# Routing weights turned and expanded by short products, GpSimd's product of unit 10 moved up, last output blocks evacuated between scans

## The chip, the cores and the metric

The kernel runs on one core of a Trainium2 chip. The metric is the device time of one execution in microseconds (us); the times before are the median of three runs. Engines are named as in the profile: PE is TensorE (PEld its weight loads), DVE is VectorE, ACT is ScalarE, POOL is GpSimd, SP is the engine that issues most DMAs.

## What is computed

The output is `x + ffn(mix(x, f, cond))`, in float32, for 4 batches of 1024 tokens by 1024 channels. The reference, cut to what matters:

```python
# mix: r = x, k = v = f, tf = sigmoid(sum(cond)) per batch
ek = exp(min(k, 30)); ekv = ek * v
nf, nb = scan(ekv), reverse_scan(ekv)          # a = a * decay + ekv_t, over the tokens
df, db = scan(ek), reverse_scan(ek)
euk = exp(min(u + k, 30))
y = sigmoid(r) * (nf + nb - ekv + euk * v) / max(df + db - ek + euk, 1e-8) * (0.8 + 0.2 * tf)
# ffn on y
h = silu(y @ rw1.T + rb1)
logits = h @ rw2.T + rb2 + gates               # 16 experts
coeff = softmax of the two largest logits, scattered to a row of 16, zero elsewhere
xa = einsum('ni,eri->ner', y, A)               # rank 16 per expert, so 256 values per token
out = x + y @ W.T + bias + einsum('ner,eor->no', xa * coeff[:, :, None], B)
```

## The kernel before

**Layout.** Everything is channel major: a tile has 128 channels on the partitions and tokens along the free dimension. A *unit* is one batch and one block of 128 channels (1024 tokens): 32 units, eight per batch, one per step `s` of the loop that every engine runs. A *group* `G` is one batch's half of 512 tokens: 8 groups; its outputs are eight blocks `j` of 128 channels.

**The recurrences (DVE, POOL, ACT).** For a unit DVE runs four scans of about 2.2 us each: forward of the denominator (L704) and of the numerator (L708), backward of both (L713, L734); and between them L718 (product with v), L723 (sum of the denominators), L692 (scaling of the next unit's exponential) and L747 (the ratio, which gives y). POOL makes the numerator's input of the next unit (`p1`, L602, which DVE's next forward scan waits for), sums the numerators (L580, after the backward scan), gates them (L586, which L747 waits for), and takes the remainder of y (L612). ACT does exponentials, sigmoids, logarithms with table loads between them, and rounds y.

**Products in three passes.** Each product is done in a rounded type (fp32r) with both operands split into a rounded part and a remainder: hi*hi, hi*lo, lo*hi. `y_hi` is ACT's, `y_lo` is POOL's (L612), and TensorE waits for `y_lo` of a unit. A 128x512 product is one instruction. ffn's output blocks accumulate in five PSUM banks; `acc` holds them.

**Routing of a group.** TensorE makes the hidden layer (`hid`, L936) and xa (`low_rank`), and then the logits (`logits`, L974). DVE's `routing` finds the two largest and their weights with some twenty small instructions, tokens on the partitions. The weights must then multiply xa, which has the 256 (expert, rank) rows on the partitions. Before, `fan_out` (L810) writes each weight 16 times, to `fan`, 128x512 twice; TensorE turns `fan` against an identity in full float32 (`spread`, L981), eight products of 128x128, which run as sixteen instructions. DVE multiplies (`weigh`, L818), ACT rounds the result (`split_wx`, L470), POOL takes its remainder (`wx_lo`, L625), and then TensorE runs `expert`. It waits for `wx_lo` before the first of them. Between `spread` and `expert` it has base products of the third output block, 24 of them in groups 2 to 7, and twelve more.

**Order.** Each engine's program is written by hand as a loop over steps, with tables that place work of groups 0 and 1 (`routing_at`, `weigh_at`, `evacs_at`) and rules for groups 2 to 7 (`quarter`, `ends_at`). Every engine runs strictly in that order and waits at semaphores. Group 0 is routed in step 9, group 1 in step 12; group G from 2 on in step 8+4G+1, and its last five output blocks are evacuated (L754, `evacuate`) in step 8+4G+4. Banks that are evacuated are taken by the next group's first products (`bank_in`).

## Time and profile before

| | |
|---|---|
| median of 3 runs | 689.52 us (688.38 to 690.01) |
| the profiled execution, its own time | 688.6 us |
| its span, first to last instruction | 686.6 us |
| PE busy | 598.7 us (87%) |
| DVE busy | 526.6 us (77%) |
| POOL busy | 368.1 us (54%) |
| ACT busy | 357.1 us (52%) |
| mean granted clock of TensorE | 0.957 |

Busy time is an average over stages. In the first 250 us or so DVE has little idle time and PE waits; later PE runs almost without a gap while DVE ends its scans at 537 us.

### The profile page before, as it was taken

The page shows a single profiled execution, that of the slowest core. Times are in us where ns is not written, and L with a number is a line of the kernel's source. Part 1 is how long each engine was busy: PE and PEld are TensorE (multiplying, and loading weights), DVE is VectorE, ACT ScalarE, POOL GpSimd, SP SyncE. Part 2 cuts the span into 40 slices and gives each one's busy share as a digit, 9 for nine tenths or more (in the row PEclk, how much of TensorE's full clock was granted, in tenths as well). Part 3 has the DMA queues.
Part 4 walks back from the last instruction along what each step waited for, and adds up shares of the span by engine and source line. Part 5 has one row for each costly group of instructions (what it writes and reads, how often), then busy time and mean ns, then how long its engine had stood idle before and what let it go on. Part 6 is the DMA issues. An engine that isn't in the chain of part 4 may idle for free.

```text
span 686.6 us, 7030 instructions
## 1 busy us (share of the span) xinstructions
PE 598.7 (87%) x2626; PEld 490.1 (71%) x2626; DVE 526.6 (77%) x573; ACT 357.1 (52%) x418; POOL 368.1 (54%) x183
## 2 busy tenths in 40 slices
PE   0153588989999937999999999999999999999997
PEld 0132466768878825887888878888888888888886
DVE  7999999999999999998899797979897532021202
ACT  4777789785656666655655554656465420011000
POOL 1789997867868876647544753565465501000100
PEclk9976799989999978999999999999999999999999
DMA  5323476522945831234423360427132402040022
GB/s 190 122 90 121 124 254 205 194 100 71 215 107 121 203 113 64 74 113 160 141 73 113 109 198 32 153 63 242 33 116 84 124 29 66 27 153 1 25 67 76
DMA packets 33169, 78.42 MB, mean 114 GB/s; under 512 B 4720, under 2 KB 4848, under 8 KB 33136
## 3 DMA queue, kind: packets, MB, share of 16 engines
q1 hardware_dynamic: 30832, 73.79, 33.2%
q0 software_dynamic: 2304, 4.20, 3.8%
q8 instruction: 20, 0.33, 0.2%
q14 instruction: 13, 0.11, 0.0%
HBM read 57.00 MB, written 20.97 MB: 114 GB/s over the span
## 4 chain that ended last, share of the span: by engine, by line
PE 49%; DVE 25%; POOL 16%; issue 7%; ACT 1%; DMA 1%; SPq 0%; DVEq 0%; POOLq 0%; ACTq 0%
PE acc L925 15%; PE acc L927 15%; PE acc L926 15%; DVE mix L713 5%; POOL mix L602 4%; POOL kv L580 4%; POOL yr L586 4%; DVE yr L747 3%; DVE mix L708 3%; DVE eu L723 3%; DVE kv L718 2%; DVE xo L754 2%; POOL y_lo L612 2%; DVE mix L734 2%; PE acc L936 1%
## 5 line engine op out<-in xcount | busy, mean ns | idle before, releaser
L925 PE MATMUL acc<-y_hi,wa_hi 128*128 128x512 f32 x640 | 258.5, 404 | 59.7 <-POOL y_lo L612 52.7
L926 PE MATMUL acc<-y_lo,wa_hi 128*128 128x512 f32 x640 | 255.3, 399 | 0.0
L927 PE MATMUL acc<-y_hi,wa_lo 128*128 128x512 f32 x640 | 254.8, 398 | 0.0
L925 PEld LDWEIGHTS acc<-y_hi,wa_hi 128*128 128x128 f32 x640 | 124.1, 194 | 89.3 <-POOL y_lo L612 54.1
L927 PEld LDWEIGHTS acc<-y_hi,wa_lo 128*128 128x128 f32 x640 | 123.8, 194 | 26.7
L926 PEld LDWEIGHTS acc<-y_lo,wa_hi 128*128 128x128 f32 x640 | 124.2, 194 | 25.6
L602 POOL TENSOR_TENSOR mix<-mix,kv 128x1024 f32<-128x1024 f32 x31 | 74.3, 2397 | 75.7 <-DVE mix L692 59.4
L754 DVE SCALAR_TENSOR_TENSOR xo<-acc,bias_sb,xo 128x512 f32<-128x512 f32 x64 | 46.4, 735 | 75.2 <-PE acc L927 75.2
L612 POOL TENSOR_TENSOR y_lo<-yr,y_hi 128x1024 fp32r<-128x1024 f32 x31 | 74.3, 2398 | 50.2 <-ACT y_hi L402 50.2
L625 POOL TENSOR_TENSOR wx_lo<-xa,wx_hi 128x512 fp32r<-128x512 f32 x16 | 20.9, 1329 | 129.3 <-ACT wx_hi L470 129.3
L580 POOL TENSOR_TENSOR kv<-mix,kv 128x1024 f32<-128x1024 f32 (+1 forms) x32 | 75.4, 2356 | 5.3 <-DVE mix L734 5.3
L704 DVE TENSOR_TENSOR_SCAN mix<-d_ps,mix 128x1024 f32<-128x1024 f32 x32 | 73.1, 2284 | 5.8 <-POOL mix L602 5.7
L414 ACT ACTIVATE mix<-mix,rdelta_g 128x1 f32<-128x1 f32 x64 | 18.6, 296 | 111.6 <-DVE mix L708 71.6
L586 POOL TENSOR_TENSOR yr<-kv,yr 128x1024 f32<-128x1024 f32 (+1 forms) x32 | 75.2, 2351 | 2.5
L713 DVE TENSOR_TENSOR_SCAN mix<-d_ps,mix 128x1023 f32<-128x1023 f32 x32 | 74.8, 2336 | 0.3 <-ACT mix L414 0.3
L734 DVE TENSOR_TENSOR_SCAN mix<-d_ps,mix 128x1023 f32<-128x1023 f32 (+1 forms) x32 | 73.7, 2303 | 0.0
L708 DVE TENSOR_TENSOR_SCAN mix<-d_ps,mix 128x1024 f32<-128x1024 f32 x32 | 72.7, 2272 | 0.0
L402 ACT ACTIVATE y_hi<-yr 128x1024 fp32r<-128x1024 f32 x31 | 32.9, 1060 | 51.6 <-DVE yr L747 51.6
L747 DVE SCALAR_TENSOR_TENSOR yr<-eu,limit_g,yr 128x1024 f32<-128x1024 f32 (+1 forms) x32 | 40.2, 1257 | 22.5 <-POOL yr L586 22.5
L925 PE MATMUL acc<-wx_hi,wb_hi 128*128 128x512 f32 x128 | 50.0, 391 | 1.8 <-POOL wx_lo L625 1.8
L926 PE MATMUL acc<-wx_lo,wb_hi 128*128 128x512 f32 x128 | 49.8, 389 | 0.0
L927 PE MATMUL acc<-wx_hi,wb_lo 128*128 128x512 f32 x128 | 49.8, 389 | 0.0
(98 smaller groups left out, 738.3 us busy)
## 6 DMA issues: line engine op xcount, KB each, us to landing
kv<-f_cm SPq DMA_DIRECT2D x32, 512.0 KB, 3.6
yr<-x_cm SPq DMA_DIRECT2D x32, 512.0 KB, 3.4
out<-xo SPq DMA_DIRECT2D x64, 256.0 KB, 4.2
xo<-x_cm SPq DMA_DIRECT2D x64, 256.0 KB, 3.9
out<-xo POOLq DMA_DIRECT2D x16, 256.0 KB, 6.8
xa<-w_base SPq DMA_DIRECT2D x5, 512.0 KB, 3.5
xo<-w_base SPq DMA_DIRECT2D x3, 512.0 KB, 5.7
xo<-w_router_a SPq DMA_DIRECT2D x2, 480.0 KB, 3.6
```

The source lines that it names most:

```text
L580: nc.gpsimd.tensor_tensor(kv[:, g % 2, t], num_of(g)[:, t], kv[:, g % 2, t], ALU.add).then_inc(n_ready, 1)
L586: nc.gpsimd.tensor_tensor(yr[:, g % 2, t], kv[:, g % 2, t], yr[:, g % 2, t], ALU.mult).then_inc(gated, 1)
L602: nc.gpsimd.tensor_tensor(num_of(g), den_of(g), kv[:, g % 2, :], ALU.mult).then_inc(p1_ready, 1)
L612: nc.gpsimd.tensor_tensor(slots(y_lo, g), yr[:, g % 2, :].rearrange("p (h t) -> p h t", h=2), slots(y_hi, g).bitcast(fp32), ALU.subtract). ...
L704: nc.vector.tensor_tensor_scan(den_of(g), decay(g, T), den_of(g), 0.0, ALU.mult, ALU.add).then_inc(den_fwd, 1)
L708: nc.vector.tensor_tensor_scan(num_of(g), decay(g, T), num_of(g), 0.0, ALU.mult, ALU.add).then_inc(num_fwd, 1)
L713: nc.vector.tensor_tensor_scan(rev(den_of(g)), decay(g, T - 1), rev(den_of(g)), den_of(g)[:, T - 1:T], ALU.mult, ALU.add).then_inc(den_bwd, 1)
L734: nc.vector.tensor_tensor_scan(a[:, stop - 1::-1], decay(g, stop), a[:, stop - 1::-1], a[:, stop:stop + 1], ALU.mult, ALU.add).then_inc(nu ...
L747: nc.vector.scalar_tensor_tensor(out=yr[:, g % 2, t], in0=eu[:, t], scalar=limit_f[:, g:g + 1], in1=yr[:, g % 2, t], op0=ALU.min, op1=ALU. ...
L925: nc.tensor.matmul(out_ap, wh, yh, start=start, stop=False)
L926: nc.tensor.matmul(out_ap, wh, yl, start=False, stop=False)
L927: return nc.tensor.matmul(out_ap, wl, yh, start=False, stop=stop)
```

## The change

The routing weights of a group are no longer written 16 times each. DVE adds the two hits into one row of 16 weights per token, writes a rounded copy of it twice and its remainder twice side by side into `cat` (128 tokens by 4x2x32), TensorE turns `cat` in the rounded type (`turn`, four products of 64 columns of weights by 128), ACT copies the result from PSUM to `cat_t` (64x512), and TensorE expands it (`spread`, two products of 32 rows by 512 columns with a constant 0/1 matrix `expand`). For groups 1 to 7 nine base products stand between `turn` and `spread`; for group 0 none. The identity and the 0/1 matrix are rounded once on ACT in step 3.

In step 9, DVE weighs xa of group 0 after the sum of the denominators instead of before it, and POOL does `p1(10)` ahead of the two `wx_lo` of group 0. The last five blocks of groups 2 to 6 are evacuated one step earlier, between the instructions of the scans (one of them at the start of the step after). `u` is read without a copy per batch.

```diff
+        last_blocks_at = {(-1, AFTER_BWD_DEN): 3, (-1, AFTER_P2): 4, (-1, AFTER_SUM): 5, (-1, AFTER_SCALE): 6,
+                          (0, AFTER_FWD): 7}
-        weigh_at = {(CB + 1, AFTER_P2): 0, (CB + 4, AFTER_RATIO): 1}
+        weigh_at = {(CB + 1, AFTER_SUM): 0, (CB + 4, AFTER_RATIO): 1}
...
@@ ACT
+            def constants():
+                act.wait_ge(late_in, 16 * 8)
+                nc.scalar.activation(ident_r[:], ident_raw, ACT.Copy).then_inc(constants_ready, 1)
+                nc.scalar.activation(expand_r[:], expand_raw, ACT.Copy).then_inc(constants_ready, 1)
+
+            def copy_turned(G):
+                act.wait_ge(turned, G + 1)
+                nc.scalar.activation(cat_t[:], acc[0:4 * E, banks[G][0], :], ACT.Copy).then_inc(cat_t_ready, 1)
...
+                if q == 1:
+                    copy_turned(G)
                 if s == CB + 4:
                     exp_gap(1)
                     copy_xa(1)
+                    copy_turned(1)
...
+                if s == 3:
+                    constants()
+                if s == CB + 1:
+                    copy_turned(0)
@@ POOL
-                if s in (CB + 1, CB + 4):
-                    split_wx((s - CB) // 4)
+                if s == CB + 4:
+                    split_wx(1)
                 if s + 1 < UNITS:
                     p1(s + 1)
+                if s == CB + 1:
+                    split_wx(0)
@@ DVE
-                for a in range(2):
-                    fan_out(a)
...
+                nc.vector.tensor_tensor(second_hit, first_hit[:, :, :], second_hit, ALU.add).then_inc(route, 1)
+                twice = second_hit.unsqueeze(2).to_broadcast([P, TPG, 2, E])
+                routed_to(11 + 2 * TPG)
+                nc.vector.tensor_copy(cat[:, :, :, 0:E], twice).then_inc(route, 1)
+                routed_to(12 + 2 * TPG)
+                nc.vector.tensor_tensor(cat[:, :, :, E:2 * E], twice, cat[:, :, :, 0:E].bitcast(fp32),
+                                        ALU.subtract).then_inc(cat_ready, 1)
...
+            def last_blocks(s, place):
+                for late in (-1, 0):
+                    G = ends_at.get(s - late, -1)
+                    if SPLIT <= G < GROUPS - 1 and (late, place) in last_blocks_at:
+                        evacuate(G, last_blocks_at[late, place])
@@ PE
-            def spread(G, a):
-                pe.wait_ge(fan_ready, 2 * G + a + 1)
-                for t in range(TPG):
-                    last = nc.tensor.matmul(acc[:, banks[G][2 * a], t * P:(t + 1) * P], fan[:, a, t * P:(t + 1) * P], ident_sb[:],
-                                            start=True, stop=True)
-                last.then_inc(c_done, 1)
+            def turn(G):
+                pe.wait_ge(cat_ready, G + 1)
+                for t in range(TPG):
+                    last = nc.tensor.matmul(acc[0:4 * E, banks[G][0], t * P:(t + 1) * P],
+                                            cat[:, t, :, :].rearrange("p a k -> p (a k)"), ident_r[:], start=True, stop=True)
+                last.then_inc(turned, 1)
+
+            def spread(G):
+                pe.wait_ge(cat_t_ready, G + 1)
+                for a in range(2):
+                    rows = slice(2 * E * a, 2 * E * (a + 1))
+                    nc.tensor.matmul(acc[:, banks[G][2 * a], :], expand_r[rows, :], cat_t[rows, :],
+                                     start=True, stop=True).then_inc(c_done, 1)
...
+                turn(G)
                 pe.wait_ge(xa_copied, 2 * G + 2)
-                for a in range(2):
-                    spread(G, a)
                 if G:
-                    for kc in range(k0, CB):
+                    for kc in range(k0, k0 + 3):
+                        base(G, 2, kc)
+                spread(G)
+                if G:
+                    for kc in range(k0 + 3, CB):
                         base(G, 2, kc)
```

On POOL, in step 9. `wb_lo` is the remainder of the last weights, `mix<-mix,kv` is `p1(10)`, and `kv<-mix,kv` the sum of unit 9's numerators. Before:

```order
L573 TENSOR_TENSOR wb_lo<-xo,wb_hi 128x1024
L625 TENSOR_TENSOR wx_lo<-xa,wx_hi 128x512 x2
L602 TENSOR_TENSOR mix<-mix,kv 128x1024
L580 TENSOR_TENSOR kv<-mix,kv 128x1024
L586 TENSOR_TENSOR yr<-kv,yr 128x1024
```

and in the changed kernel:

```order
L598 TENSOR_TENSOR wb_lo<-xo,wb_hi 128x1024
L627 TENSOR_TENSOR mix<-mix,kv 128x1024
L650 TENSOR_TENSOR wx_lo<-xa,wx_hi 128x512 x2
L605 TENSOR_TENSOR kv<-mix,kv 128x1024
L611 TENSOR_TENSOR yr<-kv,yr 128x1024
```

The product of unit 10 has gone ahead of the two remainders.

On ACT, in the same step. `ex` is the exponential of the routing, `wb_hi` the last weights, `yr<-yr` the sigmoid of unit 9 between its two table loads. Before:

```order
L465 ACTIVATE ex<-gap 128x4
L446 ACTIVATE wb_hi<-xo 128x1024
L426 ACT_TABLE_LOAD
L426 ACTIVATE yr<-yr 128x1024
L478 ACT_TABLE_LOAD
L470 ACTIVATE wx_hi<-xa 128x512 x2
```

and in the changed kernel:

```order
L472 ACTIVATE ex<-gap 128x4
L453 ACTIVATE wb_hi<-xo 128x1024
L481 ACTIVATE cat_t<-acc 64x512
L433 ACT_TABLE_LOAD
L433 ACTIVATE yr<-yr 128x1024
L496 ACT_TABLE_LOAD
L486 ACTIVATE wx_hi<-xa 128x512 x2
```

The copy of the turned weights, which waits for TensorE, stands ahead of both table loads and the sigmoid, and `wx_hi` behind them as it did.

On DVE, steps 19 and 20, where group 2 ends (`xo<-acc` is an evacuated block, `mix` a scan). Before, from the backward scan of unit 19's denominator:

```order
L713 SCALAR_TENSOR_TENSOR mix<-d_ps,mix 128x1023
L718 SCALAR_TENSOR_TENSOR kv<-eu,kv 128x1024
L723 SCALAR_TENSOR_TENSOR eu<-eu,mix 128x1024
L692 TENSOR_SCALAR mix<-mix,delta_g 128x1024
L734 SCALAR_TENSOR_TENSOR mix<-d_ps,mix 128x1023
L754 SCALAR_TENSOR_TENSOR xo<-acc,bias_sb,xo 128x512 x2
L704 SCALAR_TENSOR_TENSOR mix<-d_ps,mix 128x1024
L754 SCALAR_TENSOR_TENSOR xo<-acc,bias_sb,xo 128x512
L708 SCALAR_TENSOR_TENSOR mix<-d_ps,mix 128x1024
L754 SCALAR_TENSOR_TENSOR xo<-acc,bias_sb,xo 128x512
L747 SCALAR_TENSOR_TENSOR yr<-eu,limit_g,yr 128x1024
L754 SCALAR_TENSOR_TENSOR xo<-acc,bias_sb,xo 128x512
```

and in the changed kernel:

```order
L740 SCALAR_TENSOR_TENSOR mix<-d_ps,mix 128x1023
L781 SCALAR_TENSOR_TENSOR xo<-acc,bias_sb,xo 128x512
L745 SCALAR_TENSOR_TENSOR kv<-eu,kv 128x1024
L781 SCALAR_TENSOR_TENSOR xo<-acc,bias_sb,xo 128x512
L750 SCALAR_TENSOR_TENSOR eu<-eu,mix 128x1024
L781 SCALAR_TENSOR_TENSOR xo<-acc,bias_sb,xo 128x512
L719 TENSOR_SCALAR mix<-mix,delta_g 128x1024
L781 SCALAR_TENSOR_TENSOR xo<-acc,bias_sb,xo 128x512
L761 SCALAR_TENSOR_TENSOR mix<-d_ps,mix 128x1023
L731 SCALAR_TENSOR_TENSOR mix<-d_ps,mix 128x1024
L781 SCALAR_TENSOR_TENSOR xo<-acc,bias_sb,xo 128x512
L735 SCALAR_TENSOR_TENSOR mix<-d_ps,mix 128x1024
```

Four blocks now stand ahead of the backward scan of the numerator, where none stood, and five ahead of the ratio, where four stood.

## Rows read from the trace of the kernel before

**Rows 1.** The page: busy tenths of TensorE in 40 slices
```profile
PE   0153588989999937999999999999999999999997
```

**Rows 2.** Waits of TensorE: who waited for whom, us in total, times, longest
```profile
PE acc L925 <- POOL y_lo L612: 52.7, 4, 27.7
PE acc L936 <- POOL y_lo L612: 9.7, 2, 8.9
```

**Rows 3.** Timeline of TensorE, group 5: start, duration, row, idle before
```profile
487.12 1.06 PE L974 MATMUL acc<-rw_sb,fan 64*128 64x16 f32 x8
...
488.12 0.50 PE L925 MATMUL acc<-y_hi,wa_hi 128*128 128x512 f32 x1
...
493.69 1.95 PE L981 MATMUL acc<-ident_sb,fan 128*128 128x128 f32 x16
...
495.39 0.48 PE L925 MATMUL acc<-y_hi,wa_hi 128*128 128x512 f32 x1
```

**Rows 4.** Timeline of VectorE, step 9
```profile
147.84 1.28 DVE L810 TENSOR_TENSOR fan<-first_hit,d_ps 128x512 f32<-128x512 f32 x2
...
149.04 1.22 DVE L718 SCALAR_TENSOR_TENSOR kv<-eu,kv 128x1024 f32<-128x1024 f32 x1
...
152.81 0.74 DVE L692 TENSOR_SCALAR mix<-mix,delta_g 128x1024 f32<-128x1024 f32 x1
...
157.09 2.29 DVE L704 TENSOR_TENSOR_SCAN mix<-d_ps,mix 128x1024 f32<-128x1024 f32 x1 [1.27 <-POOL mix L602]
```

**Rows 5.** Timeline of ScalarE, steps 8 and 9
```profile
134.48 0.58 ACT L450 COPY fan<-acc 64x512 f32<-64x512 f32 x1
...
147.05 1.28 ACT L426 ACT_TABLE_LOAD   x1
...
150.91 0.63 ACT L470 ACTIVATE wx_hi<-xa 128x512 fp32r<-128x512 f32 x1 [0.21 <-DVE xa L818]
```

**Rows 6.** Timeline of GpSimd, step 9
```profile
151.62 3.07 POOL L625 TENSOR_TENSOR wx_lo<-xa,wx_hi 128x512 fp32r<-128x512 f32 x2 [2.11 <-ACT wx_hi L470]
...
154.65 2.41 POOL L602 TENSOR_TENSOR mix<-mix,kv 128x1024 f32<-128x1024 f32 x1
```

**Rows 7.** Timeline of TensorE, groups 0 and 1
```profile
139.41 1.86 PE L974 MATMUL acc<-rw_sb,fan 64*128 64x16 f32 x8 [2.45 <-DVE fan L764]
...
141.19 0.79 PE L925 MATMUL acc<-y_hi,wa_hi 128*128 128x512 f32 x1
...
149.09 1.95 PE L981 MATMUL acc<-ident_sb,fan 128*128 128x128 f32 x16
...
154.75 0.50 PE L925 MATMUL acc<-wx_hi,wb_hi 128*128 128x512 f32 x1 [0.80 <-POOL wx_lo L625]
...
197.85 1.95 PE L981 MATMUL acc<-ident_sb,fan 128*128 128x128 f32 x16
```

**Rows 8.** Stretch of TensorE after its wait at 139 us: busy, clock, DMA
```profile
141.19:149.09 7.90, 7.90 (x25) 0.69 0.40 133
```

**Rows 9.** Timeline of VectorE, step 12
```profile
192.38 0.22 DVE L775 TENSOR_TENSOR lg<-acc,rbg 128x64 f32<-128x64 f32 x1 [0.56 <-PE acc L974]
...
200.01 1.27 DVE L818 TENSOR_TENSOR xa<-acc,xa 128x512 f32<-128x512 f32 x2
```

**Rows 10.** Timeline of TensorE, first products of groups 2, 3, 4 and 6
```profile
250.09 0.79 PE L936 MATMUL acc<-y_hi,wr 128*128 128x512 f32 x1 [8.90 <-POOL y_lo L612]
...
321.77 0.50 PE L936 MATMUL acc<-y_hi,wr 128*128 128x512 f32 x1 [0.60 <-DVE xo L754]
...
404.96 0.50 PE L936 MATMUL acc<-y_hi,wr 128*128 128x512 f32 x1 [0.83 <-POOL y_lo L612]
...
548.99 0.39 PE L936 MATMUL acc<-y_hi,wr 128*128 128x512 f32 x1
```

**Rows 11.** Timeline of VectorE, step 32
```profile
537.44 2.70 DVE L754 SCALAR_TENSOR_TENSOR xo<-acc,bias_sb,xo 128x512 f32<-128x512 f32 x4
```

**Rows 12.** Timeline of GpSimd, step 32
```profile
545.05 2.39 POOL L612 TENSOR_TENSOR y_lo<-yr,y_hi 128x1024 fp32r<-128x1024 f32 x1 [2.56 <-ACT y_hi L402]
```

More of the change, by code:

```diff
@@ L8, in decay_mix_with_routed_lora_channel_major @@
 def decay_mix_with_routed_lora_channel_major(nc, x_cm, f_cm, cond, w, u, w_router_a, w_base, w_expert, bias, rb1, rw2,
-                                             rb2, gates, ident, iota, out):
+                                             rb2, gates, ident, expand, iota, out):
     fp32, fp32r, u32 = mybir.dt.float32, mybir.dt.float32r, mybir.dt.uint32
@@ L60, in decay_mix_with_routed_lora_channel_major @@
         wx_hi = nc.alloc_sbuf_tensor_at("wx_hi", [P, 2, N], fp32r, offset=fan_at)
-        ident_sb = sb("ident_sb", [P, P])
+        cat = nc.alloc_sbuf_tensor_at("cat", [P, TPG, 2, 2 * E], fp32r, offset=fan_at)
+        cat_t = nc.alloc_sbuf_tensor_at("cat_t", [4 * E, N], fp32r, offset=fan_at + 4 * N)
+        ident_r = sb("ident_r", [P, P], fp32r)
+        expand_r = sb("expand_r", [4 * E, P], fp32r)
         rw2_sb = sb("rw2_sb", [HID, E])
@@ L161, in base_from @@
             return HALF if G < SPLIT else 0
-        (AFTER_FWD, AFTER_FWD_NUM, AFTER_RATIO, AFTER_BWD_DEN, AFTER_P2, AFTER_SUM, AFTER_BWD_NUM) = range(7)
+        (AFTER_FWD, AFTER_FWD_NUM, AFTER_RATIO, AFTER_BWD_DEN, AFTER_P2, AFTER_SUM, AFTER_SCALE, AFTER_BWD_NUM) = range(8)
         hidden_at = {(CB, AFTER_BWD_NUM): 0, (CB + 3, AFTER_SUM): 1}
@@ L263, in decay_mix_with_routed_lora_channel_major @@
         ex_ready = sem("ex_ready")
-        fan_ready = sem("fan_ready")
+        cat_ready = sem("cat_ready")
+        turned = sem("turned")
+        cat_t_ready = sem("cat_t_ready")
+        constants_ready = sem("constants_ready")
         xa_done = sem("xa_done")
@@ L390, in exp_uk @@
                     act.wait_ge(y_ready, g)
-                nc.scalar.activation(eu[:], kv[:, g % 2, :], ACT.Exp, bias=u_f[:, g:g + 1]).then_inc(euk_ready, 1)
+                nc.scalar.activation(eu[:], kv[:, g % 2, :], ACT.Exp, bias=u_sb[:, g % CB:g % CB + 1]).then_inc(euk_ready, 1)
             def split_hi(g):
@@ L473, in drain_part @@
                 act.wait_ge(part_done, p + 1)
+                if p == PBUF - 1:
+                    act.wait_ge(constants_ready, 2)
                 if p >= PBUF:
@@ L490, in _ @@
             weights_hi(0)
-            act.wait_ge(u_ready, 1)
+            act.wait_ge(u_in, 16)
             for s in range(STEPS):
@@ L766, in routing @@
             def routing(G):
-                ROUTE = 10 + 2 * TPG
+                ROUTE = 12 + 2 * TPG
                 def routed_to(n):
@@ L803, in routing @@
                 routed_to(10 + 2 * TPG)
-                for a in range(2):
-                    fan_out(a)
-            def fan_out(a):
-                e = slice(a * P // RANK, (a + 1) * P // RANK)
-                wide = [P, TPG, P // RANK, RANK]
-                nc.vector.tensor_tensor(fan[:, a, :].rearrange("p (t e r) -> p t e r", t=TPG, r=RANK),
-                                        first_hit[:, :, e].unsqueeze(3).to_broadcast(wide),
-                                        second_hit[:, :, e].unsqueeze(3).to_broadcast(wide), ALU.add).then_inc(fan_ready, 1)
+                nc.vector.tensor_tensor(second_hit, first_hit[:, :, :], second_hit, ALU.add).then_inc(route, 1)
[5 more added lines that the diff above has]
+                                        ALU.subtract).then_inc(cat_ready, 1)
             def weigh(G):
@@ L859, in _ @@
                 ended = ends_at.get(s, -1)
-                ending = ended >= 0
+                ending = ended == GROUPS - 1
                 if ending:
@@ L873, in _ @@
                 first_groups(s, AFTER_FWD)
+                last_blocks(s, AFTER_FWD)
                 if ending:
@@ L907, in _ @@
                 first_groups(s, AFTER_BWD_DEN)
+                last_blocks(s, AFTER_BWD_DEN)
                 if s < UNITS:
@@ L910, in _ @@
                 first_groups(s, AFTER_P2)
+                last_blocks(s, AFTER_P2)
                 if s < UNITS:
@@ L913, in _ @@
                 first_groups(s, AFTER_SUM)
+                last_blocks(s, AFTER_SUM)
                 if s + 1 < UNITS:
                     scale_e(s + 1)
+                last_blocks(s, AFTER_SCALE)
                 if q == 0 and routed:
@@ L1034, in _ @@
                     if G == 0:
-                        pe.wait_ge(late_in, 16 * 7)
+                        pe.wait_ge(late_in, 16 * 8)
                 else:
@@ L1133 @@
         "ident": np.eye(P, dtype=np.float32),
+        "expand": np.concatenate([np.tile(h, (2, 1)) for h in np.split(np.repeat(np.eye(e, dtype=np.float32), r, axis=1), 2,
+                                                                       axis=1)]),
         "iota": np.arange(e, dtype=np.float32),
```

16 lines of the change are left out of this document (7 added, 9 removed).

## The prediction

> **What bounds the kernel now.** I read the page's slices first, then TensorE's waits, then the timelines of the places where the change acts. The slices [rows 1] show three stages: to about slice 5 TensorE works in bursts, then nearly always, with one dip at slices 14 and 15, and from there it is full to the end. The waits [rows 2] name what the bursts and the dip wait for: the remainder of y from GpSimd (L612), 52.7 us in four waits, and 9.7 us in two at the head of a group. So the first stages go at the pace of the unit chain (VectorE's scans with GpSimd between them), and that chain also sets when group 2 starts, at 250.09 after a wait of 8.90 [rows 10]. From there TensorE is the bound, with small waits: 0.60 for an evacuated block at 321.77 and 0.83 for a unit at 404.96 [rows 10].
>
> Two things follow. In groups 0 and 1 a change counts only by what it does to the unit chain. From group 2 on it counts by TensorE's own instructions, and by units that come too late.
>
> **TensorE's short products.** Before, a group's turn of the weights is sixteen instructions and the next product starts 1.70 us after their first (493.69 to 495.39) [rows 3], 0.106 each. The change puts 4 + 2 there. The two of 512 columns: 24 products between 488.12 and 493.69 [rows 3] take 0.23 each, so 0.46; 0.23 if both ran at once. The four short ones are a form the trace lacks. The nearest rows are the sixteen at 0.106 and the logits, eight at (488.12 - 487.12) = 0.125 though only 16 columns move [rows 3]. Half an 0.106 is the lower end (half the weight columns), 0.21 the upper (no gain from the type: two of today's instructions each). I take 0.11: 0.45 for four, ends 0.2 and 0.85. For changing between shapes I take 0.15 of the logits' excess, ends 0 and 0.3. Sum 1.06 (0.43 to 1.61), so a group saves 0.64 us (1.27 to 0.09).
>
> TensorEngine Tiling (Array Packing) in the Trainium skill, section Key Properties, says that changing the tiling mode drains TensorE, which speaks against splitting one block of short products into two of other shapes. The logits row, with its 0.125 for 16 columns, doesn't contradict it, and the 0.15 stands without it.
>
> **VectorE in the routing.** The two wide writes took 1.20 (147.84 to 149.04) [rows 4]. Three dependent ones of 64, 128 and 128 elements replace them: 0.4 by elements, 1.2 at most; I take 0.85. It saves 0.35 per group.
>
> **Group 0, step 9: the largest term.** Before: the turn starts at 149.09, as soon as the base products end, `wx_hi` at 150.91 [rows 5], `wx_lo` at 151.62 and the experts at 154.75 [rows 6, 7]. Now, in order:
> - `cat` is ready at 147.84 + 0.85 = 148.7; TensorE is free at 149.09, as before, and done at 149.7 with the way to PSUM.
> - ACT copies 64x512, which takes 0.58 [rows 5]: 150.3. Behind it in ACT's queue stand two table loads and the sigmoid, which ran unhindered from 147.05 and let `wx_hi` start 3.65 later (3.86 less its 0.21 of waiting) [rows 5]. So `wx_hi` starts at 150.3 + 3.65 = 153.95 and both halves are there at 155.1.
> - VectorE: from 149.04 to the scaling at 152.81 [rows 4] the same four instructions stand as now; from 148.7 with 0.2 less waiting that gives 152.3, and 153.0 when scaled.
> - GpSimd does `p1(10)`, 2.4 us [rows 6], to 155.4, and then the two remainders. They took 3.07 there; they cannot take less than the 2.4 of one full width. I take 2.7: 158.05. The experts start at 158.1 instead of 154.75, that is 3.3 later.
> - The clock. After the 2.45 us wait at 139.41 and the logits, the granted clock over the next 7.90 us was 0.69 of full, so partly at 1.2 GHz [rows 7, 8], and 24 products took 7.90 instead of 5.5. Here TensorE waits 0.7 for the copy, 0.7 for `xa`, and then nearly 4 us. The fall costs 0 to 2.4; I take 1.2. TensorE is 4.5 late.
>
> What is behind it: TensorE has no gap from there to the logits of group 1, and VectorE waited 0.56 for those at 192.38 [rows 9]. The scan of unit 10, which began at 157.09 after 1.27 of waiting for `p1` [rows 4], now begins at 155.5; but that 1.6 is lost again, first at the evacuation of group 0's first block, which needs the experts, and at the latest at those logits. So VectorE's chain is 4.5 late at 192, less 0.35 for the routing. Then `weigh(1)`: TensorE's turn at 197.85 [rows 7] + 4.5, 0.55 for turn and shape change, nine products 2.07, and 0.4 to the first result give 200.9 + 4.5; VectorE is ready at 200.01 - 0.35 + 4.5 [rows 9]. It waits 1.2. The chain is then 4.5 - 0.35 + 1.2 = 5.35 late, and has no slack up to the y that group 2 waits for. So group 2 starts 5.35 late (3.8 with the clock held, 6.6 at the other end).
>
> **Groups 2 to 7.** TensorE saves 0.64 in each, six times 3.8. The 0.60 wait at 321.77 goes, as block 3 is evacuated in time: four blocks, done within 2.7 us [rows 11], stand earlier. Its cover is that group 2's experts are done when VectorE comes by.
>
> What is late next is the unit that a group needs. In group 4 it was 0.83 late already. VectorE's steps 17 to 24 are locked to TensorE at the logits of group 3; behind these the chain gets +1.2 of waiting in `weigh`, -0.35, and one more block ahead of the ratio (0.65): 1.5. So TensorE loses 1.5 there and the saving of group 3 with it. In group 6, the last unit's y was ready at 545.05 + 2.39 = 547.44 and needed at 548.99 [rows 10, 12]. Now four blocks (2.6) stand ahead of its last scan, and +0.85 as before: 550.9. TensorE loses 1.9 and the saving of group 5.
>
> **Sum, against the profiled execution:** 5.35 - 0.60 - 0.64 (group 2) + 1.5 (to group 4) - 0.64 (4) + 1.9 (to group 6) - 1.28 (6 and 7) = +5.6 on 688.6, so 694.2; 695.1 against the median, which lies 0.9 above. I predict **694.5**, with 691 to 698 as this case's own range (the clock, the price of the short products, and units 1 us earlier).
>
> `u` without its copy, the two roundings in step 3, and one more small DMA cost nothing: the first scaling waits for ACT's exponential, and ACT has idle time in every step. With that cover gone they cost 0.2 to 0.5 once.
>
> **Rivals.**
> - *The savings count and the front does not stretch (faster).* Place: ACT's copy in step 9. If group 0's experts start less than about 0.5 us late (VectorE's slack at 192.38), the 1.6 of the scan of unit 10 and twice 0.35 stay in the chain. Then 688.6 - 2.3 - 3.8 - 0.6 + 1.2 = 683 to 685. For it: POOL and VectorE idle there before. Against: ACT's queue order and 3.65 us of table loads and sigmoid. I give it 0.22, at 685.
> - *The two expansions run at once.* They use rows 0 to 31 and 32 to 63. Then 0.23 less, seven times, as it also brings `weigh` forward: 692.9. TensorEngine Tiling (Array Packing), Key Properties, says that different tiles can execute in parallel; no row of this trace has two such tiles. Chance 0.12.
> - *Short products are not cheap* (0.21 each). Then 0.4 more in each of seven groups: 697.3. Chance 0.13.
> - *It cancels*: full clock in group 0, 3.8 there, units in time in groups 4 and 6 because the slack at the ratio takes the blocks: 688.6 + 3.8 - 0.6 - 3.8 = 688 to 690. Chance 0.10.
>
> The forecast keeps 0.43. Its neighbours on the slower side are 0.12 and 0.13. A measurement of this kernel can tell about 0.2%, 1.4 us, from no change. Faster: 0.20 of the first rival, 0.02 of the last. Same: 0.02, 0.08, and 0.05 from the forecast's and second rival's warm-clock ends, 0.15. Slower: 0.63. The range 685.5 to 698 leaves out about 0.12 of the first rival below and 0.06 above.
>
> **What would show it.** Right: `wx_lo` of group 0 starting behind `p1(10)` at about 155.4 and TensorE waiting 3 to 4 us for it; VectorE waiting 3 us or more at the first instruction of group 1's routing; about 1.2 us of waiting at `weigh` in groups 1 to 5; group 2's first product at 253 to 257; TensorE waiting 2 to 3 us for a unit in group 4 and 1 to 2 in group 6; steady groups at 71.3 instead of 71.9 us. Wrong: experts of group 0 at 156 or earlier; group 2 starting at 250 or earlier; four short products under 0.3 us or over 0.7.

## The result and the profile after

The changed kernel takes 695.94 us (median of five runs, 694.77 to 696.10) against 689.06 us (five runs, 688.38 to 690.01): a ratio of 1.0095, 95% interval 1.0081 to 1.0109. It is slower by 6.9 us, or 1%. Its profiled execution took 695.62 us, with a span of 693.5 us. All points of time below, unless said otherwise, are from the profiled executions (this one against 688.6 us with a span of 686.6 before).

The page's slices of TensorE (against [rows 1]; slices are counted from 0):

```profile
PE   0243688879999946999999989999999999999997
```

The dip at slices 14 and 15 is still there (4 and 6 for 3 and 7), and slice 23 has an 8 where a 9 stood: TensorE, full to the end before, now has a gap in group 4. Its waits (who for whom, us in all, times, longest), against [rows 2]:

```profile
PE acc L959 <- POOL y_lo L637: 53.4, 4, 27.5
PE acc L970 <- POOL y_lo L637: 16.3, 4, 9.9
PE acc L959 <- POOL wx_lo L650: 3.0, 2, 1.8
```

The wait for the first units is as it was. At the head of a group it is 16.3 us in four waits where it was 9.7 in two. The timeline of TensorE (start, duration, row, idle before) has the products that it waited for, against [rows 10]. They are not the first of their groups, as the heading of [rows 10] and the prediction call them (only the row of group 3 there is): in group 2 it is the first product of the batch's unit 6, and in groups 4 and 6 that of unit 7, the batch's last. "Group 2 starts" is kept below for the first of them.

```profile
254.88 0.80 PE L970 MATMUL acc<-y_hi,wr 128*128 128x512 f32 x1 [9.87 <-POOL y_lo L637]
...
409.19 0.50 PE L970 MATMUL acc<-y_hi,wr 128*128 128x512 f32 x1 [2.94 <-POOL y_lo L637]
...
555.75 0.50 PE L970 MATMUL acc<-y_hi,wr 128*128 128x512 f32 x1 [2.41 <-POOL y_lo L637]
```

They are 4.79, 4.23 and 6.76 us later than before. The start of each group's logits, for which the same products stand before and after, gives the shift between these points: +3.09 in group 3 (345.03 against 341.94), +5.80 in group 4 (421.00), +5.00 in group 5 (492.12), +8.49 in group 6 (567.54) and +7.68 in group 7. So two things act in turn: a late unit pushes TensorE back, and each group without one gives 0.81 us back (a period of 71.12 us, where it was 71.93). Between the late unit of group 4 and that group's logits another 1.57 us is lost, and 1.73 in group 6. The stretches of TensorE behind both units tell why; columns: window and its length, busy time (instructions), granted clock, DMA share, GB/s:

```profile
409.19:421.00 11.81, 11.81 (x45) 0.86 0.38 122
...
555.75:567.54 11.79, 11.79 (x44) 0.86 0.01 1
```

TensorE is busy all the time, but the granted clock is 0.86: part of each stretch ran at 1.2 instead of 2.4 GHz. Before, the same work took 10.24 us at 1.00:

```profile
404.96:415.20 10.24, 10.24 (x45) 1.00 0.19 60
```

The timeline of group 4 shows where in the stretch it was. From 410.22 to 413.62 eight products start 0.41 to 0.43 us apart, and behind them they start 0.23 apart again; eight times 0.20 is the 1.6 us. Two rows, one of each kind:

```profile
410.63 0.63 PE L959 MATMUL acc<-y_hi,wa_hi 128*128 128x512 f32 x1
...
413.87 0.40 PE L961 MATMUL acc<-y_hi,wa_lo 128*128 128x512 f32 x1
```

The short products, in group 5, against [rows 3]:

```profile
498.69 0.40 PE L1015 MATMUL acc<-ident_r,cat 128*64 128x128 f32 x4
498.92 0.45 PE L959 MATMUL acc<-y_hi,wa_hi 128*128 128x512 f32 x1
499.21 0.40 PE L960 MATMUL acc<-y_lo,wa_hi 128*128 128x512 f32 x1
...
500.83 0.40 PE L961 MATMUL acc<-y_hi,wa_lo 128*128 128x512 f32 x1
501.16 0.50 PE L1023 MATMUL acc<-cat_t,expand_r 32*128 32x512 f32 x2
501.59 0.50 PE L959 MATMUL acc<-y_hi,wa_hi 128*128 128x512 f32 x1
501.92 0.39 PE L960 MATMUL acc<-y_lo,wa_hi 128*128 128x512 f32 x1
```

Four turning products take 0.23 us from start to start, and the pair of expanding ones 0.43. Around them the spacing of the base products is a little wider than its usual 0.23: 0.29 behind the turn, 0.33 before and 0.33 behind the expansion. In all 0.30 us for the turn and 0.64 for the expansion, 0.94 a group. The sixteen of before took 1.70, and the product behind them stood 0.32 from the next instead of 0.23, so 1.79 in all.

Group 0, where the front comes from: ScalarE, GpSimd, VectorE and TensorE, against [rows 4 to 7]:

```profile
148.91 0.59 ACT L481 ACTIVATE cat_t<-acc 64x512 fp32r<-64x512 f32 x1 [2.29 <-PE acc L1015]
149.52 1.28 ACT L433 ACT_TABLE_LOAD   x1
150.82 1.06 ACT L433 ACTIVATE yr<-yr 128x1024 f32<-128x1024 f32 x1
151.89 1.28 ACT L496 ACT_TABLE_LOAD   x1
153.19 1.15 ACT L486 ACTIVATE wx_hi<-xa 128x512 fp32r<-128x512 f32 x2
```

```profile
152.50 2.39 POOL L627 TENSOR_TENSOR mix<-mix,kv 128x1024 f32<-128x1024 f32 x1 [3.44 <-DVE mix L719]
154.85 2.50 POOL L650 TENSOR_TENSOR wx_lo<-xa,wx_hi 128x512 fp32r<-128x512 f32 x2
```

```profile
154.93 2.29 DVE L731 TENSOR_TENSOR_SCAN mix<-d_ps,mix 128x1024 f32<-128x1024 f32 x1 [0.25 <-POOL mix L627]
160.20 0.75 DVE L781 SCALAR_TENSOR_TENSOR xo<-acc,bias_sb,xo 128x512 f32<-128x512 f32 x1 [2.98 <-PE acc L961]
```

```profile
157.41 0.62 PE L959 MATMUL acc<-wx_hi,wb_hi 128*128 128x512 f32 x1 [1.78 <-POOL wx_lo L650]
```

The copy of the turned weights ends at 149.50, and the table loads and the sigmoid behind it hold `wx_hi` back until 153.19. GpSimd's remainders follow its product, and the experts start at 157.41. The scan of unit 10 begins 2.2 us earlier than before, and VectorE then stands 2.98 us at the first evacuation.

### The profile page after: what moved, and what is told of

It reads as the page before. It is cut to its first block, busy times and chain, and to the rows that moved or that the text cites. A ratio compares the mean times of both kernels' runs of the same rounds, so it can differ in the third digit from the quotient of the medians.

```text
span 693.5 us, 6883 instructions
## 1 busy us (share of the span) xinstructions
PE 596.4 (86%) x2546; PEld 481.8 (69%) x2546; DVE 521.5 (75%) x580; ACT 361.9 (52%) x428; POOL 367.3 (53%) x183
## 4 chain that ended last, share of the span: by engine, by line
PE 51%; DVE 22%; POOL 17%; issue 7%; ACT 1%; DMA 0%; POOLq 0%; DVEq 0%; SPq 0%; ACTq 0%
PE acc L959 16%; PE acc L961 16%; PE acc L960 16%; DVE mix L740 5%; POOL mix L627 5%; POOL kv L605 4%; POOL yr L611 4%; DVE yr L774 3%; DVE eu L750 2%; POOL y_lo L637 2%; DVE kv L745 2%; DVE mix L735 2%; DVE xo L781 2%; DVE mix L731 2%; DVE mix L761 1%
```

## The experiments

The times are medians of 5 to 12 runs; the kernel before had 688.7 to 689.2 us beside them, and ratios are against it. The runs of a version spread by 1 to 5 us from lowest to highest run, so differences under 1 us say little. Two tables give all but experiments 2, 5, 6 and 10, in us ("blocks" are the last five output blocks of groups 2 to 6, which the expectations of experiments 3 and 4 call those of groups 2, 4 and 6; the edits move all five groups'):

| | last blocks in a row | blocks between scans |
|---|---|---|
| weights of before | 689.0 (before) | 694.0 |
| short products, orders of the change | 693.8 | 695.9 (after) |
| short products, both orders of group 0 mended | 690.4 | 691.7 |

| with the late units covered (below) | |
|---|---|
| before | 688.0 |
| blocks between scans alone | 687.9 |
| after | 686.1 |
| after, with the orders of group 0 mended and two units between | 683.6 |

**1. ScalarE's order in group 0**, on the changed kernel, with GpSimd's order put back too. (The expectation calls the moved work a copy of 64x512; it is `wx_hi`, two of 128x512.)

```diff
@@ ACT
                     copy_turned(0)
+                    split_wx(0)
...
-                if s == CB + 1:
-                    split_wx(0)
@@ POOL
-                if s == CB + 4:
-                    split_wx(1)
+                if s in (CB + 1, CB + 4):
+                    split_wx((s - CB) // 4)
                 if s + 1 < UNITS:
                     p1(s + 1)
-                if s == CB + 1:
-                    split_wx(0)
```

> Edit on the kernel after: for group 0 ScalarE's copy of 64x512 that splits the weighed remainder (wx) is put directly behind its copy of the turned weights, so that the two loads of activation tables and the sigmoid between come after it, and GpSimd forms the remainder of group 0 ahead of its product of unit 10, as before the change. Theory A (the late start of group 2 comes from ScalarE's order in group 0): in the kernel after, that copy started at 153.19, 4.3 us behind the turned weights' copy at 148.91; moved, it should start near 150.2-150.5, the experts' products of group 0 should start near 153.8-154.2 instead of 157.41, group 2's first product near 251.0-251.8 instead of 254.88, and the whole should come out 3 to 4.5 us under the kernel after (about 691.5-693), near 1.004 of the kernel before. Rival B (the delay is made later, in the routing steps of group 1 or by the clock, whatever the start of group 0): the experts start earlier but group 2's first product stays within 1 us of 254.88 and the time within 1 us of 695.9.

Measured: 691.74 us (690.89 to 695.74), ratio 1.005 [1.0031, 1.007], 4.2 under the changed kernel. On ScalarE and TensorE:

```profile
149.46 0.59 ACT L481 ACTIVATE cat_t<-acc 64x512 fp32r<-64x512 f32 x1 [2.29 <-PE acc L1012]
151.75 1.23 ACT L486 ACTIVATE wx_hi<-xa 128x512 fp32r<-128x512 f32 x2 [1.70 <-DVE xa L840]
153.00 1.28 ACT L433 ACT_TABLE_LOAD   x1
```

```profile
149.01 0.42 PE L1012 MATMUL acc<-ident_r,cat 128*64 128x128 f32 x4 [1.13 <-DVE cat L833]
150.20 0.49 PE L1020 MATMUL acc<-cat_t,expand_r 32*128 32x512 f32 x2 [0.77 <-ACT cat_t L481]
151.77 0.79 PE L956 MATMUL acc<-y_hi,wa_hi 128*128 128x512 f32 x1 [1.08 <-DVE xa L840]
...
251.87 0.79 PE L967 MATMUL acc<-y_hi,wr 128*128 128x512 f32 x1 [9.88 <-POOL y_lo L636]
```

`wx_hi` is 1.4 us earlier, not 3, since it now waits 1.70 for VectorE's `xa`. The experts start at 156.12, later than expected: nothing releases them any more, TensorE comes there by itself, with three waits of about 1 us in the step and seven of the twelve products behind them at half clock (0.43 apart). Group 2 starts at 251.87, 3.0 earlier than in the changed kernel's profile. Theory A holds for the place, with the start of the experts missed by 2 us. Its size is in part the clock: kernels with the changed kernel's group 0 but with the clock held behind the experts start group 2 at 253.7 (experiments 3, 5 and the third of 9), so the orders give 1.9 and that clock the other 1.1; and in group 4 the clock did not fall here behind a wait of 2.79 us (10.20 us from unit to logits), which is 1.6 more.

**2. GpSimd's order alone** (the part of that diff under POOL).

> Edit on the kernel after: only GpSimd's order is put back: the remainder of group 0 (wx_lo, two instructions) is formed ahead of the product of unit 10, as before the change; ScalarE's order stays as in the kernel after. Theory A (ScalarE's order sets the experts' start): wx_lo then waits for ScalarE's copy, which ends at 154.35, and can be done near 156.9 instead of 157.4; the experts start 0.3-0.9 us earlier, and unit 10's product about 4 us later, which puts its scan behind. The time comes out 0 to 1 us under the kernel after (695.0-695.9). Rival B (GpSimd's product standing ahead of the remainder is what delays the experts): the experts start near 154-155 and the time falls by 2.5 us or more.

Measured: 694.11 us (693.42 to 695.27), 1.8 under the changed kernel; experts at 156.83, group 2 at 252.82. The experts came 0.6 earlier, as A said; the time fell by more than A's 1 us and less than B's 2.5. Part of this may not be from the edit: the changed kernel's profiled execution lost 1.6 us more to the clock in group 0 (below). Against the 253.7 of the kernels with the clock held, group 2 starts 0.9 earlier here and 1.9 earlier in experiment 1, so each of the two orders costs about 1 us.

**3. The last blocks in a row again.**

```diff
-        last_blocks_at = {(-1, AFTER_BWD_DEN): 3, (-1, AFTER_P2): 4, (-1, AFTER_SUM): 5, (-1, AFTER_SCALE): 6,
-                          (0, AFTER_FWD): 7}
+        last_blocks_at = {}
...
-                ending = ended == GROUPS - 1
+                ending = ended >= 0
```

> Edit on the kernel after: the last accumulator blocks of groups 2, 4 and 6 are evacuated where they were before the change (in one row at the group's end), not between the scans. Theory A (the moved evacuations put the units of groups 4 and 6 off, TensorE waits 2.94 and 2.41 us for them, and its granted clock falls after both waits, 1.6-1.7 us each): the wait for a free accumulator at group 3's first product comes back (+0.6 to +0.8), the wait at group 6's unit falls under 0.7 and leaves no fall of the clock (-1.8 -1.7), the wait at group 4's unit falls by about 0.65 (-0.7), with its clock fall kept or gone (0 to -1.6): 3.0 to 5 us under the kernel after, 691-693. Rival B (the late units come from the late start of group 2 alone and the evacuations are neutral): the two waits stay as they are and the time is that of the kernel after plus 0.6-0.8, 696.6.

Measured: 693.84 us (691.98 to 695.06), 2.1 under the changed kernel, which is less than the 3 to 5 of theory A and the other way than B. The late units are gone as A said (0.78 us in group 4 and none in group 6), but another wait has come, on TensorE:

```profile
326.82 0.50 PE L969 MATMUL acc<-y_hi,wr 128*128 128x512 f32 x1 [1.23 <-DVE xo L780]
...
399.31 0.50 PE L969 MATMUL acc<-y_hi,wr 128*128 128x512 f32 x1 [1.07 <-DVE xo L780]
...
410.40 0.50 PE L969 MATMUL acc<-y_hi,wr 128*128 128x512 f32 x1 [0.78 <-POOL y_lo L636]
...
473.06 0.50 PE L969 MATMUL acc<-y_hi,wr 128*128 128x512 f32 x1 [1.20 <-DVE xo L780]
...
545.04 0.50 PE L969 MATMUL acc<-y_hi,wr 128*128 128x512 f32 x1 [0.56 <-DVE xo L780]
```

With the row kept, the 0.8 us that TensorE saves in a group makes it reach the next group's accumulators before VectorE has emptied them, and it hands the saving back there. So the two large parts of the change belong together: with the evacuations moved, no such wait is left in the changed kernel, and the short products count.

**4. The moved blocks alone**, on the kernel before.

> Edit on the kernel before: only the evacuations of the last blocks of groups 2, 4 and 6 are moved between the scans as the change does; weights, products and GpSimd's order stay as before. Theory A: the wait of 0.60 at group 3's first product goes (-0.6 to -0.8); the unit of group 4 comes 0.65 later (+0.65), that of group 6 about 2.6 later against a slack of about 1.5, so that TensorE waits there 0.7-1.7 us; sum +0.5 to +2 without a fall of the clock, up to +3.5 with one: 1.001-1.005 of the kernel before. Rival B (the moved evacuations only take the wait away): 0.6 us faster than before, 0.999.

Measured: 694.03 us (692.64 to 694.38), ratio 1.0063 [1.0048, 1.0077]: 5.0 slower, more than A's upper end of 3.5. On TensorE:

```profile
407.00 0.80 PE L950 MATMUL acc<-y_hi,wr 128*128 128x512 f32 x1 [2.45 <-POOL y_lo L615]
...
554.45 0.50 PE L950 MATMUL acc<-y_hi,wr 128*128 128x512 f32 x1 [1.78 <-POOL y_lo L615]
```

and VectorE, ahead of group 4's unit:

```profile
389.18 0.75 DVE L757 SCALAR_TENSOR_TENSOR xo<-acc,bias_sb,xo 128x512 f32<-128x512 f32 x1 [0.78 <-PE acc L941]
```

Group 4's unit is 2.04 us late. Of this 0.65 is taken for the block that now stands ahead of the ratio, 0.78 is a wait of VectorE for experts that TensorE had not finished (without the short products it comes too early), and 0.59 was there at the logits of group 3. The clock fell behind the first of TensorE's waits:

```profile
407.00:418.72 11.72, 11.72 (x44) 0.86 0.32 103
```

Behind the second, of 1.78 us, it did not (10.20 us from unit to logits). So this part alone, with no late front, costs most of what the whole change does. My 3.5 left out VectorE's wait and a slower clock in group 2 (73.53 us from logits to logits at 0.98 granted, and 71.93 in the steady state).

**5. Filler products in TensorE's waits**, on the changed kernel.

```diff
+                        if G in (4, 6) and kc == CB - 1:
+                            pe.wait_ge(evacuated, (G - 1) * CB + 7)
+                            for n in range(9):
+                                yh, _ = y_of(G, 0)
+                                nc.tensor.matmul(acc[:, banks[G][3], :], wa_hi[:, 0, 0:P], yh, start=True, stop=True)
                         unit_in(G, kc)
```

> Edit on the kernel after: in groups 4 and 6 TensorE computes nine more products of 128x512, whose result is overwritten, right before it takes the last unit (at 409.19 and 555.75 it waited 2.94 and 2.41 us there; nine products take 2.05 us). Work is added and none taken away. Theory A (the clock falls because TensorE stood still for over 2 us): the waits shrink to 0.4-0.9 us, the units come at the same time, the logits of groups 4 and 6 come 1.4-1.7 us earlier each against the kernel after, and the time falls by 2.5-3.5 us (692.4-693.4). Rival B (the slower products behind these waits have another cause than the stop, or the added products push the work behind them): no change or up to 1 us slower (695.9-697).

Measured: 691.83 us (691.26 to 693.88), 4.1 under the changed kernel, by adding work. The waits are 0.86 and 0.67, and behind them:

```profile
409.65:419.85 10.20, 10.20 (x45) 1.00 0.28 91
...
554.90:565.09 10.19, 10.19 (x44) 1.00 0.01 2
```

The same work as in the changed kernel takes 10.20 instead of 11.81 us, and 10.19 instead of 11.79. That is 1.6 us each, paid for the wait and not for the lateness. Theory A holds; the medians differ by 0.6 us more than its range, for which these two places give no reason.

**6. Two units (six base products) between turn and spread instead of three (nine)**, on the changed kernel.

> Edit on the kernel after: in groups 1 to 7 two units (six products) of the third base block instead of three (nine) stand between the turn and the spread of the weights; the third comes behind the spread. Theory A (VectorE's weighing waits for the spread, and its scans with it): the weights come 0.68 us earlier, VectorE's waits at the weighing (14.0 us in 7 in the whole kernel after) shrink by 0.6-0.7 each in groups 1 to 5, the units of groups 4 and 6 come 0.7 earlier or more, and the time falls by 0.7-1.5 us, by 1.6-3 more if a wait gets short enough to keep the clock. Rival B: six products (1.36 us) do not cover ScalarE's copy of the turned weights any more, TensorE waits 0.3-0.6 in each group at the spread, and the time stays or grows by up to 2 us.

Measured: 693.04 us (691.51 to 695.44), 2.9 under the changed kernel. Group 2 starts 0.7 earlier than in kernels with the same start of group 0 (253.05 against 253.74 in the one with filler), the wait in group 6 is 1.78 and the clock is kept there (10.20 us from unit to logits), and TensorE waits over 0.25 us for the copied weights in no group but 0. This is theory A, with one fall of the clock less than in the changed kernel.

**7. The short products nearly alone** (experiments 1 and 3 together).

> Edit on the kernel after: three parts at once, so that the short products for the weights stand nearly alone: the last blocks are evacuated in one row as before, GpSimd's order of group 0 is as before, and ScalarE's splitting copy stands directly behind its copy of the turned weights. Theory A (the 0.8 us per group that the short products free on TensorE turn into waits for the evacuated accumulators: with the row kept, TensorE waited 1.23, 1.07, 1.20 and 0.56 us at the first products of groups 3 to 6): those waits stand again, and the time is that of the kernel with the row kept (693.8) less the 3-4 us that the better start of group 0 is worth: 689.8-690.8, that is 1.001-1.003 of the kernel before. Rival B (the waits for the accumulators came from the late start of group 2): they stay at 0.6 in all, the saving of 0.8 in each of groups 2 to 7 counts, and the time is 686-687.5, faster than before.

Measured: 690.39 us (689.04 to 692.70), ratio 1.0016 [1.0003, 1.0029]. The waits for the accumulators stand at 0.97, 1.00, 1.12 and 0.76 although group 2 starts 1.9 earlier than in experiment 3: theory A. The short products do not pay without the moved evacuations.

**8. The late units covered.** In groups 4 and 6 TensorE took units 5, 6 and 7 in a row before the low-rank products of the three. Now the twelve of 5 and 6 stand ahead of unit 7, as work that is ready while the unit is late:

```diff
-                    for kc in range(first, CB):
+                    for kc in range(first, CB - 1):
                         unit_in(G, kc)
                         hid(G, kc)
                     for a in range(2):
-                        for kc in range(first, CB):
+                        for kc in range(first, CB - 1):
                             low_rank(G, a, kc)
+                    if first < CB:
+                        unit_in(G, CB - 1)
+                        hid(G, CB - 1)
+                        for a in range(2):
+                            low_rank(G, a, CB - 1)
```

with the orders of experiment 1 and the two units of experiment 6:

> A version meant to beat both. On the kernel after: GpSimd's order of group 0 as before, ScalarE's splitting copy directly behind its copy of the turned weights, two units instead of three between turn and spread, and in the even groups the low-rank products of units 5 and 6 (twelve, 2.7 us) are computed ahead of those that need unit 7. Theory A (the waits for the units of groups 4 and 6 and the falls of the clock behind them are the cost of the moved evacuations): the twelve products fill these waits, no fall of the clock follows, and the logits come when the hidden layer is done, near 8.6 us behind unit 7 instead of 10.2: 1.5 us gained by order and 1.6 by the clock in each of the two groups, with 4.2 from the start of group 0 and about 0.7 from the two units: 684-687. Rival B (the chain of the units is bound by VectorE, whatever TensorE does): the work moved only moves the wait to the logits, and the time is 689-691.

Measured: 683.58 us (682.03 to 685.12), ratio 0.9909 [0.989, 0.9928], 5.6 us faster than before. No wait of TensorE over 0.25 us is left behind group 2's logits, and the last three groups follow one another at 71.10 to 71.11 us.

**9. What of that needs the change.** The same reordering on the kernel before, on experiment 4, and on the changed kernel:

> Edit on the kernel before, nothing of the change in it: in the even groups the low-rank products of units 5 and 6 are computed ahead of those that need unit 7. It tells how much of the 5.5 us that the best version gained comes without the change. Theory A: the kernel before waited for a unit in group 4 alone (0.83 us, with no fall of the clock), so the order can give back 0.8 us and no more: 688.2-688.6, 0.999 of the kernel before. Rival B: the new order is worth as much here as behind the change (3 us for each of two groups): 683-686.

> Edit on the kernel before: the evacuations of the last blocks moved between the scans, as in the kernel with that part alone (694.0), and the low-rank products of units 5 and 6 ahead of those that need unit 7. Theory A (the moved evacuations cost by the late units and the clock behind them, and by nothing else): both waits (2.45 and 1.78 us) and both falls of the clock go, 1.5-1.7 by order and 1.5 by the clock in each group: 687.3-688.5, level with or just under the kernel before. Rival B (VectorE is loaded by the moved evacuations in another way): above 690.5.

> Edit on the kernel after, with the rest of the change as it is: the low-rank products of units 5 and 6 ahead of those that need unit 7. Theory A: about 3.2 us come back in group 4 and as many in group 6, and what is left against the kernel before is the late start of group 2 less the savings: 689-690. Rival B (the start of group 0 has to be mended first, since the late units come from it): the waits only move to the logits and the time falls by less than 4 us, 692 or more.

Measured: 688.00 us, ratio 0.9989 [0.998, 0.9998]; 687.89 us, 0.9978 [0.9968, 0.9989]; 686.05 us, 0.9962 [0.995, 0.9973]. Theory A each time, and in the last case 3 us more than it expected. There the logits of groups 3 to 7 are at 345.51, 416.79, 487.91, 559.25 and 630.37, so no more than 0.2 us is lost in groups 4 and 6. I had put the logits 8.6 us behind unit 7 from group 2, where products ran at half clock; they came 7.5 behind it and did not wait at all.

So the price of the moved evacuations is the late units and the clock behind them: covered, the kernels with and without them are level (687.89 and 688.00). The change with its own orders is then worth 2.0 us against the covered kernel before (686.05 to 688.00), and 4.4 with group 0 mended and two units between (683.58; that run was taken in another set, with the kernel before at 689.22 and not 688.69, so it may be 5). The short products with the late units covered but the evacuations in a row were not run.

**10. The two expansions taken apart**, on the best version.

```diff
-                spread(G)
+                    spread(G, (0,))
+                    base(G, 2, k0 + 2)
+                    spread(G, (1,))
```

> Edit on the best version so far (683.6, a steady period of 71.11 us): in groups 1 to 7 the two expanding products (32 rows of weights each, in different rows of the array) are taken apart, with three base products between them; the count of products stays. Theory A (side by side they run at once, 0.43 us from the first to the next product for both): each group grows by 0.2-0.35 us, the period to 71.3-71.45 and the time by 1.3-2.4 us. Rival B (they ran one after the other, and the saving of 0.81 a group has another source): the period grows by less than 0.1 and the time by less than 0.7 us.

Measured: 687.61 us (686.61 to 690.25), ratio 0.999 [0.9978, 1.0003], the last three groups at 71.73 to 71.74 us: 0.63 more a group, above both theories. In group 5:

```profile
494.16 0.40 PE L958 MATMUL acc<-y_hi,wa_lo 128*128 128x512 f32 x1
494.49 0.50 PE L1020 MATMUL acc<-cat_t,expand_r 32*128 32x512 f32 x1
494.92 0.50 PE L956 MATMUL acc<-y_hi,wa_hi 128*128 128x512 f32 x1
495.25 0.39 PE L957 MATMUL acc<-y_lo,wa_hi 128*128 128x512 f32 x1
495.48 0.40 PE L958 MATMUL acc<-y_hi,wa_lo 128*128 128x512 f32 x1
495.81 0.49 PE L1020 MATMUL acc<-cat_t,expand_r 32*128 32x512 f32 x1
```

One expansion alone has the same spacings of 0.33, 0.43 and 0.33 around it as the pair had. The second of a pair costs nothing, which is what two products at the same time look like. A full-height product of as many columns takes 0.23, so some 0.4 of the 0.64 us comes with the product's 32 rows, alone or in a pair; whether that is the way in and out or the product itself, the spacings do not separate.

## Why the prediction was right, and where its sum was not

694.5 was forecast and 695.94 measured; the case forecast was the one that came. Most of its signs stand: the remainders behind `p1(10)` (154.85 for 155.4), VectorE waiting 3.86 us at group 1's routing (3 or more), 1.17 at `weigh` in groups 1, 3, 4 and 5 (1.2; in group 2 it was 0.25), group 2 at 254.88 (253 to 257), TensorE waiting 2.94 us in group 4 (2 to 3) and 2.41 in group 6 (1 to 2), steady groups at 71.1 (71.3). Two do not: TensorE waited 1.78 us for the remainders of group 0, not 3 to 4, and the four turning products took 0.23, under the 0.3 that was named as a sign of being wrong (that sign rightly says that their price was off; the path of the work was as forecast). And 1.4 us of error on the total hides larger ones of both signs: 3.3 us that the sum left out were met by terms that were some 2 us too dear. That the total came so near is luck.

- **Group 0's step 9 (experts 3.3 late): right in the sum.** From the logits of group 0 to the experts it took 15.34 us before and 18.42 after, 3.1 more. ScalarE's queue held `wx_hi` for 3.7 us behind the copy (149.50 to 153.19), as read from [rows 5]; experiments 1 and 2 show that both orders matter. The remainders took 2.5 us instead of 2.7, and `cat` was about as counted (0.79, from 147.43 to 148.22, instead of 0.85). TensorE waited 1.78 and not 4 us for them, because its twelve products in between started late (1.07 us of waiting for `xa`) and took 4.41 us at a granted clock of 0.66.
- **The clock in group 0 (+1.2): a coin that I averaged.** From the experts of group 0 to the logits of group 1 the profiled execution of the changed kernel took 38.09 us against 36.53 before. In four other kernels with the same start (experiments 3, 5, 6 and the third of 9) it was 36.5. It is 1.6 or nothing, so the 1.2 matches neither; which of the two the other executions of the changed kernel had, their profiles would have to tell.
- **Between the logits of group 1 and group 2 (+0.85): 0.57.** The wait at `weigh(1)` is there, 1.17 us, as forecast. So the front is 3.65 us without the clock (3.08 + 0.57). In the profiled execution it is 4.79, with 1.56 for the clock and 0.42 off since group 0's logits came that much earlier there; 5.35 was too much.
- **The saving (0.64 a group): under-sized, 0.81.** The turn cost 0.30 with its share of the shape change, where 0.45 was taken without one; four products at 0.057 each, near the lower end of 0.2. The two expansions took 0.64 where 0.46 and 0.15 were counted, and the sixteen of before were worth 1.79 and not 1.70. This gives 0.85, of which the period shows 0.81. The second rival's mechanism is true, two expansions cost what one does (experiment 10), but not its gain of 0.23, since one costs more than was counted. TensorEngine Tiling (Array Packing) in the Trainium skill, section Key Properties, says both that different tiles can execute in parallel and that a change of mode drains TensorE; the traces are in line with both, with 0 us for the second expansion and some 0.4 that comes with a product of 32 rows between full-height ones, though they do not show a drain as such.
- **The wait for an evacuated block (-0.60): right**, and more than that: without the moved blocks the same wait took the saving of the next groups too (experiments 3 and 7). That cover I did not see.
- **Late units (+1.5 and +1.9): right in kind, a little dear**, 1.14 and 1.76 (from the logits of group 3 to the unit of group 4, and from those of group 5 to that of group 6).
- **The term that was missing: the price of a late unit was counted as its lateness alone.** The sum has "+1.5 (to group 4)" and "+1.9 (to group 6)" and nothing behind them. TensorE stood 2.94 and 2.41 us, and the granted clock then fell to 0.86 over the next 12 us: 1.57 and 1.73 us more, 3.3 in all. The row for it was in the prediction [rows 8], used for group 0 and not for these. Experiment 5 shows it by adding work: the waits fall under 1 us and the clock stays. Experiments 8 and 9 show it by moving work.

The profiled execution by measured terms: 4.79 - 1.70 (to the logits of group 3: the evacuation wait and group 2's saving) + 1.14 + 1.57 - 0.80 (group 4) + 1.76 + 1.73 - 1.61 (groups 6 and 7) = 6.88, and the spans differ by 6.9 (693.5 and 686.6).

The rival on the faster side (savings count, front does not stretch) failed at its named place. That its 685 lies near the best version (683.6) proves nothing for it: that version also has two units between and the order of experiment 8.

## What to carry to other kernels

A wait of the bounding engine, when that is TensorE, can be priced twice: once for its length, and once for the slower clock behind it (here 1.6 us behind waits of 2.4 to 2.9). Where a move makes a late operand later, look for work that is ready and can be put ahead of it, before judging the move. And a saving on one engine counts only if the engine that empties its buffers is ahead as well. Two edits that each lose alone (here +5.0 us for the moved evacuations, and +1.2 for the short products with group 0 mended) can gain together, once the late units are covered: here 2.0 to 4.4 us in the covered kernels, while without that cover the two together lost 6.9, and 2.7 with group 0 mended.

## What the runs showed of the hardware

- Behind TensorE's waits of 2.41 to 2.94 us at the units of groups 4 and 6, in a stream that was dense before, the granted clock was 0.86 over the next 12 us, at a price of 1.5 to 1.6 us, in seven of eight cases in the profiles (one of 2.79 us, in experiment 1, was the exception). Behind waits of 0.67 to 1.78 us there it fell in none of seven. What decides in the exception stays open.
- At the full clock, four products of 128x64 weights by 128 columns in the rounded type take 0.057 us each; before, sixteen instructions of the full type took 0.106 each, two for each product of 128x128 by 128.
- A pair of products on 32 rows each, on different rows of the array, costs 0.64 us amid full-height products, one alone 0.62 to 0.63.
- Another 1.6 us comes and goes between kernels that do the same work there. In group 2 it shows as 72.75 instead of 71.12 us from logits to logits, with 0.98 granted instead of 1.00, in kernels whose wait at group 2's logits was 1.78 us or longer, and not where it was 1.43 or less. No experiment changed that wait alone, so that it is the cause is not shown.
